# Two GroupNorms, a Hadamard mix and a three-layer channel MLP on one core: even statistics, four-product group means, and a fp32 step ahead of the hi/lo split

## The reference, cut to what matters

```
x = x + H(_gn(x))              # H: 192x192 part of a Hadamard matrix over channels, /16
h = einsum(_gn(x), W1) + b1    # over channels, per pixel
h = gelu(layernorm(h) * g1 + beta1)
h = gelu(layernorm(einsum(h, W2) + b2) * g2 + beta2)
x = x + einsum(h, W3) + b3
```

## Time and profile before

| what | us |
|---|---|
| median of 3 runs | 1090.71 (1089.01 to 1097.77) |
| profiled execution, its own time | 1090.9 |
| its span in the trace | 1089.1 |
| PE, DVE, ACT, POOL busy | 956.6, 874.7, 886.1, 655.7 |
| mean granted TensorE clock | 0.972 |

### The profile page before, as it was taken

The page is one execution under the profiler, slowest core; times in us unless marked ns, Lnnn a source line. Parts: engine busy times, 40 slices in busy tenths (PEclk is TensorE's granted clock), DMA queues, the critical chain, the costliest instruction groups (busy, mean ns, idle before and its releaser), DMA issues.

```text
span 1089.1 us, 25234 instructions
## 1 busy us (share of the span) xinstructions
PE 956.6 (88%) x9528; PEld 671.8 (62%) x9528; DVE 874.7 (80%) x1458; ACT 886.1 (81%) x2822; POOL 655.7 (60%) x492
## 2 busy tenths in 40 slices
PE   0665789998899989998999999998999999999985
PEld 0223557666676666666676676766676677677762
DVE  6487998899978998899987998889987887755541
ACT  0541798898987998989987998979887999899993
POOL 0432375666755675666665666657665767677772
PEclk9999899999998999999998999999998999999997
DMA  9503302313131313222222223122201111111112
GB/s 283 154 1 93 86 26 79 103 52 96 58 103 52 102 53 103 78 77 78 77 79 75 78 77 100 57 77 76 77 32 47 44 35 52 52 48 43 41 52 77
DMA packets 49081, 80.94 MB, mean 74 GB/s; under 512 B 5568, under 2 KB 48704, under 8 KB 48832
## 3 DMA queue, kind: packets, MB, share of 16 engines
q1 hardware_dynamic: 48960, 79.33, 23.9%
HBM read 40.77 MB, written 38.54 MB: 73 GB/s over the span
## 4 chain that ended last, share of the span: by engine, by line
PE 45%; DVE 24%; ACT 17%; POOL 10%; issue 2%; SPq 1%; DMA 1%; POOLq 0%; DVEq 0%; ACTq 0%
PE tm L380 10%; ACT z L470 8%; POOL rs L585 7%; DVE xs_lo L703 6%; DVE z L826 5%; PE tm L374 5%; PE tp L392 4%; PE hl L281 4%; PE hl L316 3%; DVE x_lo L816 3%; PE hl L242 3%; PE tm L367 3%; POOL ge_lo L594 3%; DVE X L838 2%; ACT ge_hi L499 2%; PE hl L302 2%
## 5 line engine op out<-in xcount | busy, mean ns | idle before, releaser
L585 POOL TENSOR_TENSOR rs<-ssq,neg_half 112x4 f32<-112x4 f32 x224 | 282.8, 1263 | 208.7 <-ACT z L470 208.5
L594 POOL TENSOR_TENSOR ge_lo<-ge,ge_hi 128x672 f16<-128x672 f32 x224 | 335.9, 1508 | 119.5 <-ACT ge_hi L499 117.4
L470 ACT ACTIVATE z<-tm 112x194 f32<-112x194 f32 x896 | 287.2, 348 | 65.4 <-PE tm L380 65.2
L826 DVE TENSOR_TENSOR z<-tm,rs 112x768 f32<-112x768 f32 x224 | 212.4, 948 | 96.6 <-POOL rs L585 96.6
L470 ACT ACTIVATION_READ_ACCUMULATOR z<-tm 112x1 f32 x896 | 201.1, 225 | 0.0
L483 ACT ACTIVATE ge<-tp,par 128x448 f32<-128x448 f32 x224 | 168.9, 754 | 29.2 <-PE tp L392 29.0
L499 ACT ACTIVATE ge_hi<-ge 128x672 f16<-128x672 f32 x224 | 175.8, 785 | 2.2
L392 PE MATMUL tp<-cst,z 112*128 112x112 f32 x896 | 128.1, 265 | 42.4 <-DVE z L826 42.3
L461 ACT ACTIVATE x_hi<-X,gscale 128x448 f16<-128x448 f32 x168 | 114.5, 684 | 38.4 <-DVE gshift L775 38.4
L703 DVE SCALAR_TENSOR_TENSOR xs_lo<-X,gscale,xs_hi 128x448 f16<-128x448 f32 x147 | 133.6, 937 | 9.6 <-ACT xs_hi L450 9.6
L392 PEld LDWEIGHTS tp<-cst,z 112*128 112x128 f32 x896 | 92.0, 142 | 68.4 <-DVE z L826 48.6
(11 more groups left out here) (124 smaller groups left out, 2229.8 us busy)
## 6 DMA issues: line engine op xcount, KB each, us to landing
X<-x SPq DMA_DIRECT2D x56, 448.0 KB, 3.7
out<-X SPq DMA_DIRECT2D x56, 448.0 KB, 2.7
X<-x SPq DMA_DIRECT2D x112, 112.0 KB, 3.7
out<-X SPq DMA_DIRECT2D x112, 112.0 KB, 2.8
X<-weights SPq DMA_DIRECT2D x1, 1152.0 KB, 11.7
cst<-consts SPq DMA_DIRECT2D x1, 832.0 KB, 9.6
X<-biases SPq DMA_DIRECT2D x1, 192.0 KB, 2.6
par<-params SPq DMA_DIRECT2D x1, 6.0 KB, 1.6
```

The costliest lines, as they stand in the source:

```text
L470: last = nc.scalar.activation(z[n][:, 2 * h + k, i * TW:(i + 1) * TW], tm[h][:, i, k * TW:(k + 1) * TW], ACT.Square, scale=float(C) ** -0. ...
L585: nc.gpsimd.tensor_tensor(rs[n][:, 2 * h:2 * h + 2, :], ssq[n][:, 2 * h:2 * h + 2, :], neg_half[0:TT, 0:4].rearrange("p (i k) -> p i k", i=2),
L594: nc.gpsimd.tensor_tensor(ge_lo[n][:, g % 2, :, cols], ge[n][:, :, cols], ge_hi[n][:, g % 2, :, cols], ALU.subtract).then_inc(s_ge_lo[n], 1)
L826: nc.vector.tensor_tensor(z[n][:, 2 * h:2 * h + 2, 0:2 * C].rearrange("p k (i o) -> p i k o", i=2), tm[h][:, :, 0:2 * TW].rearrange("p i ( ...
```

## The change

- **Statistics spread evenly**: from step 4 on every step takes exactly three `bn_stats` of x (unit g+17), instead of 21 in four steps of seven. `bn` gets two buffers. Pair 1's 21 blocks: ten in the first part, beside the second GroupNorm of pair 0, and eleven in step 0.
- **Pair 1's first GroupNorm in step 0**; units 7 to 13 then have their H product in steps 1 to 5 (two units in steps 2 and 4). Step 0 has none.
- **Sums in four products**: `gst`, `gmu`, `gscale` and `gshift` get a fourth column, so that `gn_means` and `h_shift` are four matmuls instead of seven; DVE does one more `bn_aggr` per GroupNorm, and `gn_shift` has three or six small operations and a copy instead of two. `gn_h_bias` has three instead of one.
- **Scaled x through fp32**: ACT writes `xsf` = scale times x in fp32 (three instructions), one DVE `tensor_copy` of 128x1344 writes `xs_hi`, and one POOL subtraction of 128x1344 writes `xs_lo`. `xsf` has one buffer. In the first part, unit 0 is split straight by ACT and DVE, POOL's subtraction is one instruction per unit, and the third product of an early unit goes to bank `tp` and not to `hl`.
- **Orders**: all four `step` lists are written anew.

```diff
+STATS_AHEAD = 2 * U + 3
+FIRST_H = {1: (7, -1), 2: (8, 9), 3: (10, -1), 4: (11, 12), 5: (13, -1)}
+FIRST_XS = {0: (-1, 7), 1: (8, 9), 2: (-1, 10), 3: (11, 12), 4: (-1, 13)}
+FIRST_STATS = {0: (42, 42), 1: (42, 52), 2: (52, 56), 3: (56, 63)}
...
-                for b, terms in enumerate((((AA, 0), (CIA, 2)), ((AA, 1), (CJA, 2)), ((AIC, 0), (AJC, 1), (CCB, 2)))):
-                    for i, (m, src) in enumerate(terms):
-                        last = nc.tensor.matmul(gp[:, 2 * b:2 * b + 2], group_mean[:, m, :], gst[n][:, :, src],
+                for at, terms in ((0, (AA, CA_)), (4, (AC_, CCD))):
+                    for r, m in enumerate(terms):
+                        last = nc.tensor.matmul(gp[:, at:at + 4], group_mean[:, m, :], gst[n][:, :, 2 * r:2 * r + 2],
...
+            def c_bank(a):
+                return ("tp0", tp[:, 0, 0:UT]) if a < U else ("a", hl[:, 0, 0:UT])
...
             def step(g):                                  # PE
                 group(g, 0, 0)
+                h_ab(h_unit(g, 0))
                 transposes(g - 2, 1, 1)
+                group(g, 0, 1)
+                h_c(h_unit(g, 0))
                 gn_means(gn2_pair(g), 1)
                 gn_means(gn1_pair(g), 0)
+                transposes(g, 0, 0)
+                group(g - 1, 1, 0)
+                transposes(g, 0, 1)
+                l3_ab(g - 2)
+                group(g - 1, 1, 1)
                 w1_shift(gn2_pair(g))
                 transposes(g - 1, 1, 0)
+                h_shift(h_shift_pair(g))
                 l3_c(g - 2)
+                h_ab(h_unit(g, 1))
+                h_c(h_unit(g, 1))
...
+            def scaled(a, b):                             # ACT
+                if b == 0:
+                    act.wait_ge(s_xs_lo, a)
+                nc.scalar.activation(xsf[:, b, :], xcols(a, b), ACT.Copy, scale=scale1(a // U, b)).then_inc(s_xsf, 1)
...
+            def xs_low(a):                                # POOL
+                pool.wait_ge(s_xs_hi, 3 * (a + 1))
+                nc.gpsimd.tensor_tensor(xs_lo[:, a % 2], xsf[:, :, :], xs_hi[:, a % 2], ALU.subtract).then_inc(s_xs_lo, 1)
...
             def step(g):
                 rstd(g, 0, 0)
                 groupnorm_rstd(gn2_pair(g), 1)
+                rstd(g, 0, 1)
+                groupnorm_rstd(gn1_pair(g), 0)
                 gelu_lo(g - 2, 1, 1)
+                xs_low(xs_unit(g, 0))
                 rstd(g - 1, 1, 0)
                 gelu_lo(g, 0, 0)
+                xs_low(xs_unit(g, 1))
                 rstd(g - 1, 1, 1)
                 gelu_lo(g, 0, 1)
                 gelu_lo(g - 1, 1, 0)
...
+            def xs_high(a):                               # DVE
+                dve.wait_ge(s_xsf, 3 * (a - U + 1))
+                dve.wait_ge(s_h, 2 * (a - 1))
+                nc.vector.tensor_copy(xs_hi[:, a % 2], xsf[:, :, :]).then_inc(s_xs_hi, 3)
```

More of the change, by code:

```diff
@@ L251, in h_shift @@
                 free("b")
[L252 to L255, removed]
+                for at, terms in ((0, (AA, CA_)), (2, (AC_, CCD))):
+                    for r, m in enumerate(terms):
+                        last = nc.tensor.matmul(gp[:, at:at + 2], h32[:, m, :], gshift[0][:, 2 * r:2 * r + 2, 0],
+                                                start=(r == 0), stop=(r == 1), skip_group_check=True)
                 last.then_inc(s_gred, 1)
@@ L283, in h_ab @@
                 for r, part in enumerate(parts):
-                    for i, m in enumerate((CIA, CJA)):
+                    for i in range(2):
                         rows = slice(64 * i, 64 * i + 64)
-                        last = nc.tensor.matmul(hl[:, i, 0:UT], h16[rows, m, :], part[rows, 2, :], start=False,
+                        last = nc.tensor.matmul(hl[:, i, 0:UT], h16[rows, CA_, :], part[rows, 2, :], start=False,
                                                 stop=(r == 1), skip_group_check=True)
@@ L318, in l3_ab @@
                 for r, (w, act) in enumerate(terms):
-                    for i, m in enumerate((CIA, CJA)):
+                    for i in range(2):
                         rows = slice(64 * i, 64 * i + 64)
-                        last = nc.tensor.matmul(hl[:, i, 0:UT], w[rows, m, :], act[rows, 2, :], start=False,
+                        last = nc.tensor.matmul(hl[:, i, 0:UT], w[rows, CA_, :], act[rows, 2, :], start=False,
                                                 stop=(r == 2), skip_group_check=True)
@@ L335, in l3_c @@
                 for r, (w, act) in enumerate(terms):
-                    for i, m in enumerate((AIC, AJC)):
+                    for i in range(2):
                         cols = slice(64 * i, 64 * i + 64)
-                        last = nc.tensor.matmul(hl[cols, 0, 0:UT], w[:, m, cols], act[:, i, :], start=False,
+                        last = nc.tensor.matmul(hl[cols, 0, 0:UT], w[:, AC_, cols], act[:, i, :], start=False,
                                                 stop=(r == 2), skip_group_check=True)
@@ L884, in _ @@
             gn_shift(0, 0)
+            for b in range(3):
+                scaled_lo(0, b)
             gn_h_bias(0)
+            weight_means()
             for c in range(U):
@@ L902, in _ @@
             gn_stats(0, 1)
+            stats_x(range(21, 27))
             gn_var(0, 1)
+            stats_x(range(27, 28))
             gn_shift(0, 1)
-            for b in range(3):
-                scaled_lo(U, b)
+            stats_x(range(28, 31))
             for b in range(3):
@@ L909, in _ @@
             gn_w1_bias(0)
-            for b in range(3):
-                residual(U, b)
-                stats_x1(U, b)
-            for b in range(3):
-                scaled_lo(U + 1, b)
             run(step)
```

306 lines of the change are left out of this document (162 added, 144 removed).

## The result

The changed kernel takes **1261.95 us** (median of 4 runs, 1260.71 to 1262.97) where the kernel before took 1093.79 beside it (1089.01 to 1097.77): a ratio of 1.154 (1.148 to 1.160). The forecast was 1028 with a range to 1067, so it missed by 234 us and on the wrong side. The profiled span is 1260.7 us.

A forecast was written before the change was run, and what follows sets the result against it. DVE was taken to bound the four of seven steps with x's statistics, PE and ACT the other three. The sum 1090.9 - 27.5 + 7 - 66.2 + 48u, with u = 0.5, gave 1028 us, range 998 to 1067.

The forecast's parts named there:

- A: Stage up to step 0's first product, 108.25 us before: to start near 80.7, a change of -27.5 (-18 to -30.5).
- The DVE and POOL terms of the steady state: Per pair: DVE 111.44 to 98.4 us, POOL 79.87 to 99.0; copy 0.86 us, subtraction 2.73.
- B: Stage of steps 0 to 4, to 184.6 us before: +7 + 5u, bounds 0 and +15.
- u: Cost per step of POOL's subtraction in the new queue order: between 0 and 2.73 us, taken as 0.5.
- the sum's 15.25: Steady state: us per step without statistics of x, PE and ACT full; a period is 7 x (15.25 + u) + 4.1.
- (b): Rival: DVE and POOL lock each other out, DVE 17.1 us per step, u = 1.3, 1067 us; chance 0.17.
- The cover: Steady steps: rstd 1.4 us late behind the subtraction, part of it covered by PE and ACT work that can run first.
- The lower end: Steady steps: u = 0, the subtraction finds cover, 1004 us; as a rival, chance 0.18.
- the wait at the GroupNorms: Steady state: PE's idle time at the GroupNorms, and the clock's fall with it, taken as gone.
- No stretch of clock 0.50 at the second GroupNorms: Sign: the 1.2 GHz stretch at a pair's second GroupNorm, 6.8 us before, was to vanish.
- (c): Rival: POOL's line sets the step, u = 2.73, 1135 us; chance 0.03 slower by over 1%, 0.04 about even.
- (d): Rival: DVE's copy takes 1.54 us instead of 0.86, u = 0.9, 1047 us; chance 0.1.

The follow-up runs named there:

- even: Kernel before with only the even spread of x's statistics (second buffer for them): 1060.51 us, ratio 0.970.
- old_orders: Changed kernel without the fp32 step and with the four step lists of the kernel before; first part, even statistics and four products stay: 1043.11 us, ratio 0.956.
- one_input: split_behind with gn_shift's small operations rewritten to one SBUF tensor input each, the other as pointer scalar: 1118.52 us, ratio 1.024.
- after: The changed kernel itself, with the whole change against the kernel before: 1261.95 us, ratio 1.154.
- no_fp32: Changed kernel with the fp32 step undone from unit 7 on, all orders kept: 1154.00 us, ratio 1.055.
- orders: Changed kernel with the edits of no_fp32 and one_input together (no fp32 step, first split moved behind, one-input gn_shift): 1084.39 us, ratio 0.992.
- split_behind: Changed kernel with DVE's first x1_split_lo moved behind normalise and final_ab: 1167.73 us, ratio 1.068.
- the three-part kernel: Changed kernel with POOL's subtraction of 1344 columns issued as three of 448, back to back: 1247.21 us, ratio 1.145.
- fp32_old: old_orders plus the fp32 step, with POOL's subtraction at the end of its step: 1281.68 us, ratio 1.174.

## Why the prediction was wrong

**The first part (A) was right as a sum, and in part by luck.** Step 0 starts at 78.4 us, forecast 80.7. Units 0 and 1 came 1.5 and 1.0 us later than worked out; the later units took 3.39 us each (50.07 to 53.46) instead of 4.4. PE's matmuls follow each other every 0.19 us there and not every 0.37 as in the same part before (the granted clock is listed as 1.00 in both stretches), and so DVE's three residuals and three statistics set the pace, 1.13 us a pair from start to start and not the 1.3 behind my lower bound of 3.9. Nor was the shared bank the whole of the 5.95 us of before. Its chain of waits has four statistics of pair 1 in each unit, which the change takes out:

```profile
48.99 2.10 DVE bn L689 x4
```

**The DVE and POOL terms of the steady state were right in size**: copy, subtraction, and that the four steps with statistics were bound by DVE (even: 15.2 us floor, period 116.8). The four products, for which I had counted 2.5 us of PE's time per pair, gave nothing.

**Steps 0 to 4 (B) were undersized.** Forecast +7 with bounds of 0 and 15. With the old lists back, in old_orders, the stretch to unit 8 is 20 us longer than before, 17 longer than in even: above the upper bound. The steps with extra units and statistics run at 21.5 to 22.6 us there, and I had only added up DVE's work, and that too low: by the lists, steps 0 to 4 have 14 more statistics and seven copies for five units of `scaled_lo`, not 11, eight and six, which makes +7.4 and not +3.6. What of it waits for what was not taken apart by a run.

**The step that failed is u**, the cost per step of the new orders and the subtraction, bounded by 0 and 2.73 us, taken as 0.5. The plain steps take 19.1 us against the sum's 15.25, so u is 3.8 there, above the bound.

*The upper end.* The subtraction's own length was to be the most a step can pay. But the wait is that of whoever meets the row. I named the collision, as a rule that speaks against the change and as rival (b): four operations meet POOL, two wait 1.5 us, 3.0 us per step. Its sum was nearly right: in the period 583.8 to 734.0, `x_lo` has 29.0 - 21 x 0.68 = 14.7 us too much, `gmu_b` 5.3 and `gshift` 4.4 + 1.9 - 9 x 0.15 = 4.9 (`gshift` beside `gmu_b`: 1.91 for six), in all 24.9 or 3.6 per step. What was wrong is where it was booked. I charged it to DVE's sum, 14.1 + 3.0 = 17.1, of which DVE's slack would absorb a part. In fact it sits on one split at the head of `normalise` and in one chain at the GroupNorm, on the path: with the split moved the period falls from 149.8 to 136.2 us, and with the one-input form to 127.3, so 22.5 of the 24.9 us were on it.

*The cover.* I had found the power 1.4 us late behind the subtraction and taken part of that as covered. With the held operations gone (one_input) the plain steps take 16.5 us, 1.3 more than 15.25, and the subtraction stands in their loop: hardly any of the 1.4 is covered. This is read from the chain; no run of its own tests it.

*The lower end.* The runs do not show it wrong. The new lists never ran free of every collision, but their loops, less the one wait that stands in each, are 15.08 (the 18.16 of after, and no_fp32) and 15.25 us (orders): no more than the 15.25 that the sum has at u = 0. What makes some loops of the changed kernel 19.7 us long stays open.

**The second step that failed is the wait at the GroupNorms, put at nothing.** A period less seven plain steps should have been 4.1 us. It is 16.2 in the changed kernel (whose two GroupNorm steps have no held split), 20.5 in split_behind, 11.6 in one_input, 10.5 in orders, and 10.6 in even with the old lists. The one-input form is worth 8.9 of it; another 6 to 7 us above the forecast are there in every version. "No stretch of clock 0.50 at the second GroupNorms" was wrong with it. PE idles through the held addition, and the granted clock is 0.50, the 1.2 GHz level, just behind it (window of the changed kernel, against the last row):

```profile
518.00:522.00 4.00, 1.52 (x7) 1.30 (x8) 3.97 (x8) 2.25 (x4) 1.28 (x1) 0.50 0.00 0
```

**In sum**, after against the forecast, in the cuts of the table: to step 0 -2, to unit 8 +25, five periods +177, five plain steps +17, the rest +20. Of the periods' +177, 112 went with the two edits against held DVE operations (748.9 to 636.6); 65 are left in one_input, and 42 in orders, which has the held power instead of the fp32 step.

Of the rivals, (b) named the mechanism and gave it a third of its price. (c), the only slower one, had the right sign. Its loop through POOL's subtraction is not that of the changed kernel, where POOL waits 423 us for ACT z over the span; it is the one that is left in one_input, and costs 1.3 us a step there and not 2.73. (d) did not occur: the copy takes 0.853 us. The check that I had set for (b), that `x_lo` averages well over its lone duration, does show it. The lower end of the range was slightly off in itself: 1004 with A at its better bound is 1001, not 998.

On the Trainium skill: SBUF — State Buffer, section "SBUF: two separate sides", says that a DVE operation with two SBUF inputs and a GpSimd operation that reads SBUF exclude each other, for the whole instruction. The runs agree on who is held: `x_lo` and the four-column addition are; `normalise`, with one input from PSUM, is not (0.959 us at the most in 224), nor is the form with pointer scalars (one_input). They disagree on how long: 3.08 us at the split, 5.4 at the addition, over the ends of instructions. An estimate by that page, the rest of one subtraction, would give the held split a wait of 0.9 us here (561.06 to 561.95).

## What to carry over

Before work is moved to POOL, list the DVE operations with two SBUF inputs that can arrive in its row of back-to-back instructions, price each at the rest of the row, and put behind them nothing that a chain needs; do the same for POOL's instructions against a row of such DVE operations (0.94 us per plain step in orders); moving two lines was worth 94 us here, and giving the operation one tensor input 49. Book such a wait to the loop it stands in, not to the engine's sum. And take a bundle apart: the even statistics alone gave 3.0%, with the new first part 4.4%, while the new orders, with the held power that stands in them, took 4% away.

## What was new about the hardware

- A DVE operation held by POOL can stay held over the ends of POOL's instructions while the next is ready: 3.76 us over three, 5.09 over three, 4.04 over four. A 448-column split that came into a row never got in between in these rows. Four-column operations sometimes did: the addition in the three-part kernel ended at 509.71 while its row went on, and the one in the changed kernel only after its third instruction. The row went on there too, with a power at 516.86. What opens the gap is not settled.
- It holds the other way round: POOL's power took 1.95 us, 0.94 too much, beside three two-input subtractions of DVE in a row, and got its turn only behind the last (orders).
- Size is no protection: the addition of 128x4 took 5.58 us.
- The copy of 1344 columns from fp32 to fp16 (0.853 us, 0.861 at most in 49) was never seen held, but that is no test: all 49 started while no POOL instruction ran. POOL waits for it instead: the GroupNorm's power beside it takes 1.58 us (copy at 510.09, power at 510.24), and 1.01 in fp32_old.
- POOL copies 1344 columns from fp32 to fp16 in 1.34 us and subtracts them in 2.74.
